# Four graph-attention layers: chain steps of a chunk moved behind later tiles, one centring product, and totals between the last two products

## The reference, cut to what matters

```python
def _gat(h, adj, W, a):                       # one attention layer
    Wh = h @ W
    e = (Wh @ a_src)[:, None] + (Wh @ a_dst)[None, :]
    e = leaky_relu(e, 0.2)
    att = softmax(where(adj > 0, e, -9e15), axis=1)
    return elu(att @ Wh)

x = x + _gat(relu(layernorm(x)), ...)         # l = 0, then l = 1
h = relu(layernorm(x))                        # third block
h1 = 0.2 * h + 0.8 * _gat(h, ...)             # l = 2
h2 = 0.2 * h + 0.8 * _gat(h1, ...)            # l = 3
x = x + concat(h, h1, h2) @ mlp_w + mlp_b
```

## Time and profile before

| | us |
|---|---|
| median of 3 runs | 607.5 |
| lowest and highest run | 606.79 and 609.07 |
| the profiled execution's own time | 606.7 |
| its span, first to last instruction | 604.9 |
| TensorE busy (matmul) | 533.1, 88% |
| VectorE busy | 393.1, 65% |
| ScalarE busy | 290.3, 48% |
| GpSimd busy | 31.8, 5% |

### The profile page before, as it was taken

The page is one execution under the profiler, slowest core; times in us unless marked ns, Lnnn a source line. Parts: engine busy times, 40 slices in busy tenths (PEclk is TensorE's granted clock), DMA queues, the critical chain, the costliest instruction groups (busy, mean ns, idle before and its releaser), DMA issues.

```text
span 604.9 us, 7603 instructions
## 1 busy us (share of the span) xinstructions
PE 533.1 (88%) x3144; PEld 197.7 (33%) x3144; DVE 393.1 (65%) x545; ACT 290.3 (48%) x314; POOL 31.8 (5%) x29
## 2 busy tenths in 40 slices
PE   5579998898999998998888998999769799999997
PEld 3412223343223334323233223245332234433332
DVE  2988789528989437989646989534999986101000
ACT  1477964344665443656433656435858776000000
POOL 0500000201000101000000000022000000000000
PEclk9787999999999999999999999999998899999999
DMA  8968000000000000000000000000000000000000
GB/s 323 365 223 282 26 1 1 0 2 1 0 1 1 1 1 2 1 1 0 1 1 1 1 2 1 0 1 2 0 0 1 0 2 0 1 1 1 1 2 33
DMA packets 5491, 19.42 MB, mean 32 GB/s; under 512 B 592, under 2 KB 592, under 8 KB 5456
## 3 DMA queue, kind: packets, MB, share of 16 engines
q1 hardware_dynamic: 5312, 18.11, 8.2%
q10 hardware_dynamic: 144, 0.82, 0.4%
HBM read 18.40 MB, written 0.52 MB: 31 GB/s over the span
## 4 chain that ended last, share of the span: by engine, by line
PE 53%; DVE 29%; ACT 8%; issue 6%; POOL 1%; DMA 1%; POOLq 0%; DVEq 0%; ACTq 0%
DVE X L1278 11%; PE X L997 9%; PE PROD L767 9%; PE X L759 7%; PE PROD L997 7%; PE S L787 6%; DVE aB L1540 6%; ACT big L439 5%; DVE big L1290 2%; DVE nadj L1557 2%; ACT big L485 1%; PE M L626 1%; PE M L721 1%; DVE big L1287 1%; DMA cst<-in_cst 1%
## 5 line engine op out<-in xcount | busy, mean ns | idle before, releaser
L439 ACT ACTIVATE big<-X,v 128x1024 f32<-128x1024 f32 x128 | 141.7, 1113 | 117.1 <-PE X L759 116.6
L1278 DVE SCALAR_TENSOR_TENSOR X<-wB,v,aB 128x1024 f32<-128x1024 f32 x128 | 163.4, 1292 | 19.2 <-ACT big L439 17.8
L767 PE MATMUL PROD<-big,Wh 128*64 128x512 f32 x512 | 135.1, 612 | 1.5 <-ACT big L439 1.3
L759 PE MATMUL X<-nadj,bigI 128*64 128x512 bf16 x512 | 79.1, 389 | 27.0 <-DVE X L1278 26.3
L759 PEld LDWEIGHTS X<-nadj,bigI 128*64 128x64 bf16 x512 | 24.7, 110 | 113.5 <-DVE X L1278 86.8
L787 PE MATMUL S<-big,onesf 128*32 128x512 f32 x400 | 53.3, 604 | 3.0 <-DVE big L1290 2.4
L767 PEld LDWEIGHTS PROD<-big,Wh 128*64 128x64 f32 x512 | 31.8, 137 | 53.9 <-issue 30.4
L997 PE MATMUL PROD<-big,Wh 128*64 128x512 f32 x128 | 34.0, 654 | 8.3 <-ACT big L554 8.3
L372 POOL TENSOR_TENSOR rr<-var,mhalf 128x8 f32<-128x8 f32 x8 | 17.2, 2154 | 315.8 <-DVE var L1139 315.8
L997 PE MATMUL PROD<-nadj,Wh 128*64 128x512 f32 x128 | 29.1, 598 | 0.4 <-ACT nadj L554 0.4
L997 PE MATMUL X<-big,Wh 128*64 128x512 f32 x128 | 28.6, 595 | 0.0
(11 more groups left out here) (291 smaller groups left out, 573.7 us busy)
## 6 DMA issues: line engine op xcount, KB each, us to landing
big<-in_adjT SPq DMA_DIRECT2D x28, 512.0 KB, 6.8
aB<-in_adjT SPq DMA_DIRECT2D x4, 512.0 KB, 7.7
cst<-in_cst ACTq DMA_DIRECT2D x1, 800.0 KB, 5.5
x<-in_xT SPq DMA_DIRECT2D x1, 512.0 KB, 6.2
out<-x SPq DMA_DIRECT2D x2, 256.0 KB, 2.0
late<-in_late SPq DMA_DIRECT2D x1, 272.5 KB, 4.9
```

The costliest lines, as they stand in the source:

```text
L439: act.activation(prob[:, t % U, :], X[t % 2][:], ACT.Exp, bias=v2[l % 2][:, k:k + 1]).then_inc(p_ready, 1)
L759: last = pe.matmul(X[t % 2][feat(side), hh * BANK:(hh + 1) * BANK], bigI[:, feat(side)], nadj[:, k, half_cols(c, hh)], start=False, stop=T ...
L767: last = pe.matmul(PROD[c][feat(hh), :], Wh[l % 2][:, k, :], prob[:, t % U, hh * BANK:(hh + 1) * BANK], start=k == 0, stop=k == NB - 1)
L1278: dve.scalar_tensor_tensor(X[t % 2][:], wB[:, cols(c)], v8[l % 2][:, k:k + 1], aB[:, cols(c)], ALU.max, ALU.add).then_inc(x_written, 1)
```

## The change

On VectorE, within chunk 1's tiles: `shifted` moves from tile 8 to 7 and `activated` from 9 to 8; `clip` moves from 10 to 13 and `variance` from 11 to 15 (layer 3: `mlp_rows` 10 to 11, `clip` 12 to 13, `variance` 13 to 14); `features`, `block_levels`, `feature_rows` move from tiles 13 to 15 to behind the loop, ahead of `row_parts`; the reach steps of layer 2 move from 7, 9, 12 to 8, 11, 14. `rising` comes before `falling` for chunk 1, with the two waits that `falling` has. In layer 3 `keys` is cut in two, and the reciprocals of chunk 1 stand between the halves. On TensorE: chunk 0's centring in layers 0 and 1 becomes one product of `center` and the new x, one pair later; variances, the reach spread and features each move one pair later; the totals of chunk 1 stand between the products of tiles 14 and 15; the row products of chunk 0 come after the reciprocal rows. On ScalarE: the square moves from tile 9 to 11, and `elu_exp` of chunk 1 goes ahead of `w_row`.

```diff
@@ -524,16 +524,16 @@
                         sum_copy(l, 0)
                     if k == 6:
                         elu_exp(l, 0)
-                    if k == 9 and l < 2:
+                    if k == 11 and l < 2:
                         square(2 * l + 2)
                     if k == 11 and l == 3:
                         square(2 * GAT - 2)
                     if k == 13 and l == 3:
                         centred_copy(0)
                 sum_copy(l, 1)
+                elu_exp(l, 1)
                 if l < 3:
                     w_row(2 * l + 2)
-                elu_exp(l, 1)
                 if l < 2:
                     square(2 * l + 3)
                 if l < 3:
@@ -629,6 +629,10 @@
                 out = EB[n % 2][:]
                 if n < 2:
                     pe.matmul(out, center, x[:, n, :], start=True, stop=True).then_inc(d_psum, 1)
+                elif n % 2 == 0:
+                    pe.wait_ge(p_copied, n - 1)
+                    pe.wait_ge(x_new, n - 1)
+                    pe.matmul(out, center, x[:, 0, :], start=True, stop=True).then_inc(d_psum, 1)
                 else:
                     pe.wait_ge(rp_ready, n - 1)
                     pe.matmul(out, center, rp, start=False, stop=False)
@@ -881,6 +885,10 @@
                         if c and p == NB // 2 - 1:
                             pe.wait_ge(p_ready, NB * (NCH * l + c + 1))
                             sums(l, c, k + 1)
+                            products(l, c, k)
+                            total(l, 1)
+                            products(l, c, k + 1)
+                            continue
                         if l == 0 and c == 0:
                             products(0, 0, k)
                             products(0, 0, k + 1)
@@ -900,10 +908,9 @@
                             products(l, c, k + i)
                             if p < NB // 2 - 1:
                                 mask(l, c, k + 2 + i)
-                            elif c == 0:
+                            else:
                                 mask(l, 1, i)
-                        if c == 0 or p < NB // 2 - 1:
-                            sums(l, c, k + 1)
+                        sums(l, c, k + 1)
                         if c == 0:
                             if p == 0 and l:
                                 w_broadcast(2 * l + 1)
@@ -914,19 +921,17 @@
                             total(l, 0)
                         if p == 1:
                             reciprocal_rows(l, 0)
-                            if l < 2:
-                                centre_old(2 * l + 2)
                         if l < 2:
-                            if p == 3:
+                            if p == 4:
                                 centre(2 * l + 2)
-                            if p == 4:
+                            if p == 5:
                                 variances(2 * l + 2)
                         if l < 3:
                             if p == 2 and l == 2:
                                 reach_row()
-                            if p == 3 and l == 2:
+                            if p == 4 and l == 2:
                                 reach_spread()
-                            if p == 5:
+                            if p == 6:
                                 if l == 2:
                                     pe.wait_ge(reachsq_ready, 1)
                                 features(2 * l + 2)
@@ -940,12 +945,11 @@
                                 centre_again(0)
                             if p == 6:
                                 keys(0)
-                total(l, 1)
+                if l == 3:
+                    repeat(X[0], 2)
+                reciprocal_rows(l, 1)
                 if l < 3:
                     w_rows(2 * l + 2)
-                else:
-                    repeat(X[0], 2)
-                reciprocal_rows(l, 1)
                 if l < 2:
                     centre_old(2 * l + 3)
                     early_levels(l + 1, 0, 2)
@@ -1303,6 +1307,9 @@
                 dve.scalar_tensor_tensor(om, pS, 0.0, EA[c][:], ALU.min, ALU.mult).then_inc(om_ready, 1)
 
             def rising(l, c):
+
+                dve.wait_ge(rec_psum, NCH * l + c + 1)
+                dve.wait_ge(p_copied, NCH * l + c + 1)
                 signal(dve.scalar_tensor_tensor(rp, pS, 0.0, EA[c][:], ALU.max, ALU.mult), rp_ready, NCH * l + c + 1)
 
             def shifted(l, c):
@@ -1344,7 +1351,7 @@
                 link(dve.tensor_tensor(var[:, b], var[:, b], rr[:, b], ALU.mult))
                 dve.tensor_scalar(var[:, b], var[:, b], 1e-24, None, ALU.max).then_inc(var_ready, 1)
 
-            def keys(c):
+            def keys_scaled(c):
 
                 dve.wait_ge(r_ready, 8 + 2 * c)
                 b = slice(CB * c, CB * (c + 1))
@@ -1358,6 +1365,9 @@
 
                 dve.tensor_tensor(new[:, :, :, 0, :], raw[:, :, :, 0:EMB], spread(ffk), ALU.mult)
                 link(dve.tensor_tensor(new[:, :, :, 1, :], raw[:, :, :, EMB:], spread(ff), ALU.mult))
+
+            def keys_split(c):
+
                 link(dve.tensor_copy(parts[:, :, :, 0, :], kq[:]))
                 link(dve.tensor_tensor(kqr[:], kq[:], parts[:, :, :, 0, :], ALU.subtract))
                 link(dve.tensor_copy(parts[:, :, :, 1, :], kqr[:]))
@@ -1487,43 +1497,43 @@
                     if l == 2:
                         if k == 1:
                             reach_maximum()
-                        if k == 7:
+                        if k == 8:
                             reach_diagonal()
-                        if k == 9:
+                        if k == 11:
                             reach_square()
-                        if k == 12:
+                        if k == 14:
                             reach_bound()
-                    if k == 8:
+                    if k == 7:
                         shifted(l, 0)
                     if l < 3:
-                        if k == 9:
+                        if k == 8:
                             activated(l, 0)
                     if l < 2:
-                        if k == 10:
+                        if k == 13:
                             clip(2 * l + 2)
+                        if k == 15:
+                            variance(2 * l + 2)
+                    if l == 3:
                         if k == 11:
-                            variance(2 * l + 2)
-                    if l < 3:
+                            mlp_rows(0)
                         if k == 13:
-                            features(2 * l + 2)
-                            block_levels(l + 1, 0, CB)
-                        if k >= 14:
-                            feature_rows(2 * l + 2, k - 14)
-                    if l == 3:
-                        if k == 10:
-                            mlp_rows(0)
-                        if k == 12:
                             clip(6)
-                        if k == 13:
+                        if k == 14:
                             variance(6)
+                if l < 3:
+                    features(2 * l + 2)
+                    block_levels(l + 1, 0, CB)
+                    for i in range(2):
+                        feature_rows(2 * l + 2, i)
+                    row_parts(2 * l + 2)
+                else:
+                    norms(0)
+                    keys_scaled(0)
+                reciprocals(l, 1)
                 if l == 3:
-                    norms(0)
-                    keys(0)
-                if l < 3:
-                    row_parts(2 * l + 2)
-                reciprocals(l, 1)
+                    keys_split(0)
+                rising(l, 1)
                 falling(l, 1)
-                rising(l, 1)
                 if l >= 2:
                     shifted(l, 1)
                 if l == 2:
@@ -1594,7 +1604,8 @@
             norms(1)
             maxima(0, 1)
             first_rows(0)
-            keys(1)
+            keys_scaled(1)
+            keys_split(1)
             for k in range(2, CB):
                 maxima(0, k)
             first_rows(1)
```

## The result

| | before | changed |
|---|---|---|
| median of the runs (us) | 608.15 (4 runs) | 598.53 (4 runs) |
| lowest and highest | 606.79 and 609.07 | 597.11 and 600.09 |
| profiled execution (us) | 606.7 | 598.86 |
| its span | 604.9 | 597.1 |

The ratio is 0.984, with a 95% interval of 0.9809 to 0.987: faster by 9.6 us, where 12.3 were forecast. The two profiled executions differ by less (606.7 and 598.86, or 7.8), because the one of before lies 1.45 under its median.

A forecast was written before the change was run, and what follows sets the result against it. The prediction saw TensorE (busy 88%) and VectorE (65%) stopping for each other in the second chunks. Gains of 3.9 + 3.9 + 2.5 + 2.0 = 12.3 us in layers 0 to 3 gave 595.2 us, range 591 to 600.

The forecast's parts named there:

- VectorE's three waits and TensorE's four mask waits: Layer 0, second chunk: VectorE's waits at clip, variance and features go; masks of tiles 11, 12, 14, 15 wait no more.
- Tile 9's wait: Layers 0 and 1: both elementwise steps ahead of tile 9's exponents hold its mask until 103.89, a loss of 0.47 us.
- One centring product: TensorE, layers 0 and 1: one product costs 1.06 us in pair 4, replacing 1.92 behind pair 3; dropping old-x gains 0.
- Totals between the products: End of chunk 1: column totals between the last two tiles' products cost 0.98 us, bounds 0 to twice 1.05.
- Layer 0: From pair 3 to the end of the next centring: 27.47 us against 31.38, a gain of 3.9 us.
- Layer 3: Freed tiles give 0.8 us, key splits behind the reciprocals 1.2 us; 2.0 us together.
- Layer 2, inside the chunk: Of 5.83 us of TensorE waiting, 0.74, 0.55 and 0.50 stay at tiles 9, 12 and 15; a gain of 4.0.
- Layer 2, the step that failed: Layer 2's end: TensorE waits 1.8 us for the row copy, features start at 316.60 instead of 319.15, gaining 2.5 us.
- Rival 3: TensorE's clock falls to 1.2 GHz at the gap before tile 6, layers 0 and 1: 20.5 us lost, 615.7; chance 0.03.
- Rival 1: VectorE's block behind tile 15 is late, not hidden: wholly uncovered 7.5 us in three layers, 602.7; partly, 598 to 601; chance 0.14.
- Rival 2: Only removed TensorE work pays, the waits reappear at other tiles: 3.8 us gained, 603.7; chance 0.04.
- Rival 4: The waits move with the steps and the end stays within 0.5%: 607; chance 0.03.

The follow-up runs named there:

- The later places alone: Changed kernel with three centring products, totals behind both products, row copy and row products first, `falling` first, keys unsplit, all as before: 597.34 us, ratio 0.9816.
- the row copy first: Changed kernel with ScalarE's `w_row` copy ahead of `elu_exp` again: 595.34 us, ratio 0.9795; timed again, 593.82 us, ratio 0.9777.
- the first profile: Changed kernel as it is, its first profiled execution, before any follow-up edit: 598.86 us.
- the gap filled: Changed kernel with eight more bf16 products, whose result nobody reads, ahead of layer 2's row broadcast: 596.8 us, ratio 0.9818.

## Why the prediction was right, and where it was wrong

The time fell inside the range (598.53 in 591 to 600) but 3.3 above the forecast, and the reduction was 9.6 for 12.3.

- **VectorE's three waits and TensorE's four mask waits** in layer 0: right, one by one. From layer 0's totals to layer 1's are 89.08 us, where 88.5 were forecast and 92.47 it was. The later places alone carry 10.3 of the 12.9 us that the whole change gives up to the MLP mark, both with the row copy first.
- **Tile 9's wait**: forecast 0.47, it was 0.56 (104.00 against 103.44), and taking it away gave 0.58 to 0.74. This loss stood in my own sum, and was avoidable.
- **One centring product**: 0.87 each, measured 0.86 and 0.87; the dropped old-x product worth 0, right.
- **Totals between the products**: the sum took the row's step of 0.98; it was 0.99, and the product behind them started 0.91 before the next group, for 0.93. The bounds of 0 and twice 1.05 were far too wide. What their place between the products hides is 0.42 in three layers and 0.79 in layer 3.
- **Layer 0** gave 3.40 for 3.9. The second centring ended 3.76 earlier; then VectorE's second variance came 1.52 after its products began, 1.17 in layer 1, and features waited 0.24. That 0.36 is in eleven of the twelve profiles of changed forms, all but the one with only the places moved (1.17). The row copy, the single product and the place of the totals are not its cause, since forms with and without each of them have it; the cause stays open.
- **Layer 3**: 1.96 for 2.0, by the steps described (0.78 of it by the places alone, 0.8 forecast). VectorE's reciprocals stand ahead of the splits (397.46), and the key rows follow the last split:

```profile
397.46 0.21 DVE L1300 RECIPROCAL rec<-S 128x8 f32<-128x8 f32 x1
...
399.57 0.21 DVE L1382 COPY Qst<-parts 128x192 bf16<-128x192 bf16 x1
```

```profile
399.83 0.65 PE L851 MATMUL M<-identb,Kst 128*96 128x128 bf16 x8
```

- **Layer 2, inside the chunk**: the three waits forecast to be left (0.74, 0.55, 0.50 before tiles 9, 12 and 15) are there, each a little longer. In the profile without the fall these masks start 0.80, 0.61 and 0.59 later than in an undisturbed pair (the brackets show 0.17 less, since merged busy times are longer than the steps):

```profile
284.72 0.62 PE L763 MATMUL X<-nadj,bigI 128*64 128x512 bf16 x4 [0.63 <-DVE X L1282]
...
291.82 0.62 PE L763 MATMUL X<-nadj,bigI 128*64 128x512 bf16 x4 [0.44 <-DVE X L1282]
...
297.45 0.62 PE L763 MATMUL X<-nadj,bigI 128*64 128x512 bf16 x4 [0.42 <-DVE X L1282]
```

- **Layer 2, the step that failed**: "the features ... at 316.60 instead of 319.15: 2.5 us". The wait for the row copy was forecast (1.8, measured 1.99), and where the clock held, 2.23 of the 2.5 came. What this step put at nothing is the clock behind that wait, 2.63 us in the first profile; for a new stretch at the lower clock the forecast had only "some 1 us more", in its range. Rival 3 looked for the fall before tile 6 of layers 0 and 1. There the gap grew to 1.83 (layer 0) and 1.35 (layer 1), and the clock stayed at 1.00 in every profile:

```profile
97.11 0.62 PE L763 MATMUL X<-nadj,bigI 128*64 128x512 bf16 x4 [1.83 <-DVE X L1282]
```

The clock fell at the other long gap instead, which the forecast had worked out itself. With this gap it fell in four of six profiles and cost 1.05 to 2.63 us. Without it, with the row copy first or the gap filled, it fell in none of seven, nor in before. Had the gap no part in it, all four falls would be among those six of the 14 profiles only once in 67 times. So the gap very probably makes the fall possible; what decides in one execution stays open.
- The Trainium skill, Perfetto Trace Analysis, "Matmul Optimizations", asks for matmuls back to back in batches, because TensorE's power follows its use. The traces agree in layer 2, in four of the six profiles with the gap, and not at the 1.83 us gap before tile 6.
- **Attention stage**: untouched, yet 194.2 to 196.3 over the profiles, -1.25 to +0.92 to before, so the forecast's "1.2 either way" was nearly right. It goes with where the clock falls there. Counted from the MLP mark, the five profiles of 194.2 to 194.3 us have none of it at the lower level from 71 us to 192 (one of them none before 193), and the other nine have: until 75 to 76 in the five of 194.8 to 195.4, and until 77 to 78 in the four of 196.0 to 196.3. No experiment changed this alone. Windows of the first profile show 0.68 and 0.64 of the clock in 470 to 480, 69 to 79 behind its mark:

```profile
470.00:475.00 5.00, 3.63 (x14) 2.01 (x16) 4.97 (x5) 2.35 (x3) 0.00 (x0) 0.68 0.00 0
475.00:480.00 5.00, 5.00 (x23) 2.58 (x20) 3.46 (x5) 0.82 (x1) 0.00 (x0) 0.64 0.00 0
```

Rival 1 (VectorE's block late) is out: the reciprocal was ready 0.5 us before TensorE could use it. Rival 2 (only removed TensorE work pays) is out: with nothing removed from TensorE, the places gave 10.3. Rival 4 (the end stays within 0.5%) is out by the time itself.

## What to carry to other kernels

When two engines stop for each other, move a chain step behind the later tile at which its input is there anyway, and put what is left of the wait where no tile is held by it. When a forecast finds a new idle stretch on TensorE, price the slower clock behind it too, and compare both cures: against the execution with the fall, closing the gap gave 4.2 us and filling it 2.6; against those without it, 1.5 and nothing. Compare such kernels between marks inside the program, not by spans: here start and attention stage scatter by more than most of the edits were worth.

## What the runs showed that I had not expected

An idle stretch of 1.98 us in front of the same instruction cost nothing more in one execution and 2.63 us in another of the same kernel. And with eight products more, whose result is thrown away, layer 2 took no longer than in the executions without the fall (88.72), and 2.63 us less than in the one with it. The fastest form measured is the changed kernel with the row copy first and the new x behind tile 9: 591.52 us, ratio 0.9722 to before.
